# Scaling of two blocks' values on VectorE, gathers ahead of the read tree at two block ends, rows of MLP tiles 2 and 3 ahead of the last scatter

## The chip, the cores and the metric

The kernel runs on one core of a Trainium2 chip. A core has TensorE (PE in the profile) for matmuls, VectorE (DVE), ScalarE (ACT) and GpSimd (POOL) for elementwise work, and SyncE (SP), which here does nothing but issue DMAs. Each engine works through its own program in order and waits on semaphores that others raise. The metric is the device time of one execution in microseconds. Before the change it is 1930.82 us, the median of 3 runs (1924.5 to 1932.3).

## The reference

One transformer layer over x of 16 sequences of 512 tokens with 256 features. The input is normalised once to xn, and then

- out = x + attention layer(xn) + mixture of experts(xn).
- The attention layer normalises again, forms q, k, v and two gates beta and g per head (16 heads of 16), and runs a recurrence over the 512 tokens: S = S·g; S = S + beta·k (v − kᵀS)ᵀ; o = qᵀS, where k is divided by its norm. Then come the projection Wo, a residual, a layer norm and an MLP of width 1024 with gelu.
- The mixture routes each token to 8 of 64 experts (at most 128 slots an expert), each expert a gated MLP 256 → 192 → 256; the weighted rows are added per token, with a shared expert beside them.

All is float32. The recurrence is the sequential part: 512 steps, each on a state of 16 × 16 for each of 256 pairs of sequence and head.

## The kernel before, in words

**Tiles and blocks.** Time is cut into 8 blocks of 64 tokens and each block into 8 iterations of 8 steps, so the main loop runs I = 0 to 63 on every engine. The 256 pairs lie on 128 partitions in two groups G. In each iteration VectorE does the 8 steps of the recurrence (`step`, lines 1123 to 1138: four instructions for a group, eight for a step). GpSimd forms the outputs of the iteration (`reads`): a product of the states with q over half an iteration (L827, 128x2048), and then a tree of additions (L835, L836, L837, L841). Beside it one token tile of something else is carried along: for I = 1 to 16 routing, for I = 19 to 34 (X0 to X1) four experts an iteration, from I = 35 (FILL) on the MLP of 64 token tiles.

**Expert iterations.** With n = I − 19, GpSimd gathers the token rows of the next four experts (`gather(n + 1)`, L862, four indirect DMAs) at the start of its iteration, and scatters the four results of the experts by adding to DRAM (`scatter`, L869). Each scatter waits until the one before it has landed (`sc_done`). A gather waits for `slots_ready`, the slot list, which VectorE computes in `finish_round` one round an iteration at step 1, and for the four results of the iteration whose buffer it takes. TensorE multiplies, ScalarE evacuates, and VectorE forms the product of each expert's two halves (`product`, L1062) after steps 2, 3, 5 and 6. Where `summed(I)` holds, the second half of an iteration's outputs has its tree on VectorE instead (L1175, reading what GpSimd put in `rx`, L849); at the last iteration of a block (I = 23 and 31) both trees are on GpSimd.

**Block ends.** Before block k + 1 can start, its keys are scaled by the inverse norm `rk` (`key_factors`, L1045), and its values and gates are scaled: `value_factors` (L802, 128x128), `scale_values` (L808, 128x1024, one for each group) and `scale_gates` (L816, L818). GpSimd does these at j = 6 and j = 7 of the block, ahead of that iteration's reads. VectorE waits for three increments of `vals_ready` and then copies the first keys (L1056). At j = 7 GpSimd also stores the block's outputs to DRAM (`o_d`, L973), behind the trees; the first read of the next block waits until that store has landed (L825).

**The start of the MLP.** At I = 35 SyncE runs `first_rows`: it loads the rows of tiles 0 and 1 (`back_rows`: L572 from `xw_d`, L582 twice from `o_d`) and the weights w2, waits for all 64 scatters, loads the sums of tiles 0 and 1 (`back_sums`, L592), then the rows of tiles 2 and 3, and raises `rows_free`, for which the first gelu waits. TensorE's `back_attn(i)` (L1756) needs the rows of tile i; VectorE's `back_x1(i)` (L1099) takes what it gives, for tile 2 after step 2 of I = 36; `back_sum(i)` (L1106) ends a tile. GpSimd computes each tile's inverse deviation between its reads (`back_rstd`, L903, L751, L905).

The order on each engine is written out by hand in the loops. Nothing reorders it.

Of the kernel before, what the change touches and what calls it, by code (L numbers as in the profile page):

```python
# [23 lines left out]
ALU = mybir.AluOpType  # L24
# [6 lines left out]
P = 128  # L31
B, T, D = 16, 512, 256
H, DH = 16, 16
DC = D // P
BLK = 64
NBLK = T // BLK
ST = 8
NB2 = B // 2
# [113 lines left out]

def sums_on_vector(k):
    return X0 <= (k - 1) * NB2 + 3 <= X1


ROUNDS_END = R1 + NR - 1
# [19 lines left out]
def layer(nc, x, Wq, Wk, Wv, Wb, Wg, Wo, bo, ln1_g, ln1_b, ln2_g, ln2_b, w1, b1, w2, b2,  # L177
          router_wT, w_gate, w_up, w_down, ws_gate_up, ws_down, out):
    ctx = ExitStack()
    with ctx:  # L180
# [294 lines left out]
        def _(sp):  # L475
# [108 lines left out]
            def back_rows(i):  # L584
                back_rows_x(i)
                back_rows_o(i)
# [30 lines left out]
            def first_rows():  # L617

                sp.wait_ge(y_done, UNITS_R + E)
                for i in range(2):  # L620
                    back_rows(i)
                sp.dma_start(w2_s, w2.rearrange("(c p) n -> p c n", p=P)).then_inc(mlp_ld, 16)
                sp.wait_ge(sc_done, 16 * E)
                for h in range(BUF):
                    for r in range(RT):
                        sp.wait_ge(g_ld[h][r], 16 * (E // RT // 2))
                for i in range(2):
                    back_sums(i)
                for i in range(2, 4):
                    back_rows(i)  # L630
                sp.sem_inc(rows_free, 1)

            for I in range(NI):
# [69 lines left out]
        def _(pool):  # L703
# [218 lines left out]
            for I in range(NI):  # L922
                h, j, n, k, i = I % 2, I % NB2, I - X0, I // NB2 + 1, I - R0
                if I == R1:
                    g.tensor_copy(w_s[:, :, BLK], slot_col[:, 1:2].to_broadcast([P, E])).then_inc(base_ready, 1)
                if 1 <= i <= NRT:
                    residual(i - 1)
                    route_lowered(i - 1)
                back_roots(I, 0)
                if X0 <= I and I + 1 < X1:  # L930
                    gather(n + 1, (n + 1) % 2)
                if X0 < I <= X1:
                    scatter(n * RT - 1, 3, 1 - h)
                if k < NBLK and j in (3, 4) and not sums_on_vector(k):
                    square_sums(k, j - 3)
                if k < NBLK and j == 6:
                    value_factors(k)
                    scale_values(k, 0)
                if k < NBLK and j == 7:
                    scale_values(k, 1)  # L940
                    scale_gates(k)
                if X0 <= I < X1:
                    reads(I, h, 0, j, lambda: scatter(n * RT, 0, h))
                    scatter(n * RT + 1, 1, h)
                    if summed(I):
                        products(I, h)
                        scatter(n * RT + 2, 2, h)
                    else:
                        reads(I, h, 1, j, lambda: scatter(n * RT + 2, 2, h))
                else:  # L950
                    reads(I, h, 0, j, lambda: back_roots(I, 2))
                    if 1 <= i <= NRT:
                        route_weights(i - 1)
                    back_roots(I, 1)
                    if I == X0 - 1:
                        for i in range(BUF):
                            pool.wait_ge(r_stored[i], 64 * NB2)
                            pool.wait_ge(w_stored[i], 32 * NB2)
                        pool.wait_ge(zero_st, 32)
                        gather(0, 0)  # L960
                    if I + 1 < NI:
                        reads(I, h, 1, j)
                    if 1 <= I <= 1 + LATE:
                        front_factors(I + 3)
                        route_factors(I + 3)
                if h == 1:
                    relink()
                if I == NI - 1:
                    pool.wait_ge(last_read, 2)
                if j == NB2 - 1 and I < SEG[2]:  # L970
                    pool.wait_ge(x_sums, 2 * sums_before(I))
                    for s in range(2):
                        g.dma_start(o_st[I // NB2, s], oblk[:, s].rearrange("p v t -> p (v t)")).then_inc(o_stored, 16)  # L973
                if I >= SEG[2] and (I + 1) * ST % PT == 0:
                    n = (I - SEG[2]) * ST // PT
                    for s in range(2):
                        g.dma_start(ol_st[n, s], oblk_l[:, n, s].rearrange("p v t -> p (v t)")).then_inc(o_stored, 16)
# [7 lines left out]
        def _(dve):  # L985
# [61 lines left out]
            def square_sums(k, s):  # L1047

                dve.wait_ge(sq_ready, k * 2 + s + 1)
                dve.wait_ge(rk_ready, k)  # L1050
                v.tensor_reduce(n2[:, s, :], sq[:, :].rearrange("p (t d) -> p t d", d=DH), AX.X, ALU.add).then_inc(n2_ready, 1)

            def stage_keys(L, G):

# [159 lines left out]
            first_keys()  # L1214
            relink()
            t_ = [0]

            def body(I, h, at, m_):
                j = I % NB2
                dve.wait_ge(prod_done, I * 2)  # L1220
                for s in range(ST):
                    step(I, h, s, at, m_)
                    if s == 4 and j in (3, 4) and I // NB2 + 1 < NBLK and sums_on_vector(I // NB2 + 1):
                        square_sums(I // NB2 + 1, j - 3)
                    if s == 5 and j == 5 and I // NB2 + 1 < NBLK:
                        key_factors(I // NB2 + 1)
                    r = {2: 0, 3: 1, 5: 2, 6: 3}.get(s)
                    if r is not None and (R0 <= I < R1 or X0 <= I < X1):
                        product((I - R0 if I < R1 else I - X0 + NRT) * RT + r, r)
                    if 1 <= I <= 1 + LATE and s >= 5:  # L1230
                        late_stats(I + 3, s - 5, t_)
                    if s >= 6 and summed(I - 1):
                        read_sum(I - 1, s - 6)
                    if R0 + 1 <= I <= R1 and s in (0, 1, 2, 6):
                        {0: top_values, 1: top_marks, 2: top_mask, 6: top_sums}[s](I - R0 - 1)
                    if I == R1 + 1 and s == 0:
                        prefix()
                    if finish_at(I, s) is not None:
                        finish_round(finish_at(I, s))
                    if I == FILL and s == 2:  # L1240
                        dve.wait_ge(mlp_bias, 1)
                        v.tensor_tensor(b1_s[:, :], LG[:, 0:MC], b1_in[:, :], ALU.add).then_inc(mlp_bias, 1)
                    i = sum_at(I, s)
                    if i is not None:
                        back_sum(i)
                    i = x1_at(I, s)
                    if i is not None:
                        back_x1(i)
# [711 lines left out]
```

## Time and profile before

| | before |
|---|---|
| median of 3 runs | 1930.82 us |
| the profiled execution's own time | 1931.82 us |
| its span, first to last instruction | 1930.1 us |
| DVE busy | 1742.8 us, 90% |
| POOL busy | 1587.7 us, 82% |
| PE busy | 1436.1 us, 74% |
| ACT busy | 909.1 us, 47% |
| mean granted TensorE clock | 0.832 |

The durations below are from the one profiled execution. Expert iterations run from about 600 to 1110 us of its span (VectorE busy 482.26 of 510 us there), the MLP with the rest of the recurrence from there to the end.

### The profile page before, as it was taken

The numbers are of one execution on the slowest core, as the hardware profiler recorded it, in microseconds if no ns is written. First come the engines' busy times: TensorE is split into PE (matmuls) and PEld (weight loads), VectorE is DVE, ScalarE is ACT, GpSimd is POOL, SyncE is SP. The second block draws the span as 40 slices with busy tenths as digits, with TensorE's granted clock in tenths as the row PEclk, the third lists the DMA queues.
The fourth block names the chain that finished last, engine by engine and source line by source line (L and its number), as shares of the span: only waits on it lengthen the run. The fifth ranks groups of instructions, "written<-read, shape, count | busy, mean of one in ns | idle before, by whom it ended". The sixth has DMA issues, their size and how long they took to land. (4 is left out here: it accounts for less than half of the span.)

```text
span 1930.1 us, 31359 instructions
## 1 busy us (share of the span) xinstructions
PE 1436.1 (74%) x8802; PEld 1247.6 (65%) x8802; DVE 1742.8 (90%) x4967; ACT 909.1 (47%) x2609; POOL 1587.7 (82%) x1343
## 2 busy tenths in 40 slices
PE   6776777877854577667665668988898988789738
PEld 5665666766743566556554557877777877668637
DVE  3599999999999999999987988989999999988970
ACT  4545455556544644555542445555554454334303
POOL 5469999898998888788897788889898999897851
PEclk9878778878875788788776779999999999989868
DMA  8575345534456657855658322242223311111120
GB/s 174 149 178 116 69 97 125 133 75 96 95 124 150 155 132 164 217 132 130 165 132 222 74 61 64 84 118 69 57 60 102 87 54 49 57 50 49 40 53 13
DMA packets 337169, 201.24 MB, mean 104 GB/s; under 512 B 208227, under 2 KB 327717, under 8 KB 336997
## 3 DMA queue, kind: packets, MB, share of 16 engines
q1 hardware_dynamic: 318724, 168.43, 35.5%
q0 software_dynamic: 15616, 30.55, 7.2%
q8 instruction: 71, 1.16, 0.3%
q14 instruction: 102, 0.83, 0.1%
q10 hardware_dynamic: 2656, 0.26, 0.1%
HBM read 127.58 MB, written 71.60 MB: 103 GB/s over the span
## 5 line engine op out<-in xcount | busy, mean ns | idle before, releaser
L827 POOL TENSOR_TENSOR rp<-S,qs 128x2048 f32<-128x2048 f32 x113 | 519.8, 4600 | 89.3 <-DVE S L1138 63.7
L1123 DVE SCALAR_TENSOR_TENSOR vwin<-S,gwin,bank 128x256 f32<-128x256 f32 x1024 | 483.7, 472 | 0.3
L1138 DVE SCALAR_TENSOR_TENSOR S<-S,gwin,bank 128x256 f32<-128x256 f32 x1024 | 483.1, 472 | 0.3
L1128 DVE TENSOR_REDUCE nu<-vwin 128x16 f32<-128x272 f32 x1024 | 438.1, 428 | 0.3
L1132 DVE TENSOR_TENSOR bank<-nu,bank 128x256 f32<-128x256 f32 x1024 | 430.6, 421 | 0.6
L1773 PE MATMUL bank<-region 128*128 128x128 f32 x2048 | 288.2, 301 | 0.0
L1773 PEld LDWEIGHTS bank<-region 128*128 128x128 f32 x2048 | 273.1, 214 | 18.7 <-issue 18.0
L835 POOL TENSOR_TENSOR r<-rp 128x1024 f32<-128x1024 f32 x113 | 274.3, 2428 | 7.0
L1653 PE MATMUL bank<-xaT,wqkvg 128*128 128x128 f32 (+1 forms) x1792 | 242.1, 288 | 11.1 <-ACT xaT L1312 8.0
L1784 PE MATMUL bank<-region 128*128 128x256 f32 x1024 | 234.7, 383 | 0.0
L1653 PEld LDWEIGHTS bank<-xaT,wqkvg 128*128 128x128 f32 (+1 forms) x1792 | 216.2, 190 | 25.5 <-ACT xaT L1312 11.6
L1462 ACT ACTIVATE region<-bank,b_s 128x128 f32<-128x128 f32 x512 | 145.0, 364 | 176.3 <-PE bank L1773 176.0
L1784 PEld LDWEIGHTS bank<-region 128*128 128x128 f32 x1024 | 193.2, 194 | 24.4
L1688 PE MATMUL bank<-gT,region 128*96 128x128 f32 x1024 | 156.6, 317 | 56.4 <-ACT gT L1392 42.4
L1688 PEld LDWEIGHTS bank<-gT,region 128*96 128x96 f32 x1024 | 144.0, 196 | 72.0 <-ACT gT L1392 53.4
L1397 ACT ACTIVATE sgu<-bank 96x256 f32<-96x256 f32 x128 | 48.6, 380 | 232.6 <-PE bank L1688 223.1
L1688 PE MATMUL bank<-gT,wsgu_s 128*96 128x128 f32 x1024 | 151.0, 311 | 0.0
L836 POOL TENSOR_TENSOR r<-r 128x512 f32<-128x512 f32 x113 | 143.5, 1270 | 8.9
L869 POOL DMA_INDIRECT acc_d<-region,idx_i x64 | 101.7, 1589 | 53.0 <-issue 37.0
L1688 PEld LDWEIGHTS bank<-gT,wsgu_s 128*96 128x96 f32 x1024 | 140.0, 193 | 0.0
L1324 ACT ACTIVATE stg<-bank 128x128 f32<-128x128 f32 x384 | 76.5, 282 | 117.8 <-PE bank L1653 108.5
L1697 PE MATMUL bank<-region,hg_s 96*128 96x256 f32 x256 | 78.5, 434 | 47.9 <-DVE hg_s L1062 36.4
(158 smaller groups left out, 2329.6 us busy)
## 6 DMA issues: line engine op xcount, KB each, us to landing
qkv_d<-stg SPq DMA_DIRECT2D x192, 128.0 KB, 2.3
region<-in_L_ffn_w_gate SPq DMA_DIRECT2D x64, 192.0 KB
region<-in_L_ffn_w_up SPq DMA_DIRECT2D x64, 192.0 KB
region<-in_L_ffn_w_down SPq DMA_DIRECT2D x64, 192.0 KB
region<-in_L_attn_x SPq DMA_DIRECT2D x16, 512.0 KB, 7.6
region<-in_L_attn_x SPq DMA_DIRECT2D x32, 256.0 KB, 4.8
xw_d<-region SPq DMA_DIRECT2D x32, 256.0 KB, 3.5
acc_d<-region SPq DMA_DIRECT2D x32, 256.0 KB, 4.1
```

The lines of the kernel that those rows point to most:

```text
L827: g.tensor_tensor(rp[:, :, :].rearrange("p (a v) d -> p a v d", v=DH), S[h][:, lo:lo + HS].rearrange("p t s (v d) -> p (t s) v d", v=DH), ...
L835: link(g.tensor_tensor(r1[:, :, :], rp[:, :, 0:8], rp[:, :, 8:16], ALU.add))
L836: link(g.tensor_tensor(r1[:, :, 0:4], r1[:, :, 0:4], r1[:, :, 4:8], ALU.add))
L1123: m[G] = mark(v.scalar_tensor_tensor(products_of(I, s, G)[0], earlier(h, s, G).rearrange("p (v d) -> p v d", v=DH), gwin[:, I // NB2 & 1, ...
L1128: m[G] = mark(v.tensor_reduce(nu[:, G], products_of(I, s, G)[1], AX.X, ALU.add))
L1132: m[G] = mark(v.tensor_tensor(outer[G].rearrange("p (v d) -> p v d", v=DH), nu[:, G].unsqueeze(2).to_broadcast([P, DH, DH]), key(s, G), AL ...
L1138: ins = v.scalar_tensor_tensor(S[h][:, s, G], earlier(h, s, G), gwin[:, I // NB2 & 1, G, 1, t:t + 1], outer[G], ALU.mult, ALU.subtract)
L1462: last = a_.activation(mid[i % 2][:, m, :], (G0, G1)[half][:, n * P:(n + 1) * P], ACT.Gelu, bias=b1_s[:, m:m + 1])
L1653: last = mm(dst[0:n, :], wqkvg[:, c, i * P:i * P + n], xaT[h][:, c, :], start=(c == 0), stop=(c == DC - 1))
L1688: last = mm(bk[0:FH, i * P:(i + 1) * P], w[:, c, (i % 2) * FH:(i % 2 + 1) * FH], gT[:, c, :], start=(c == 0), stop=(c == DC - 1))
L1773: last = mm((G0, G1)[half][:, n * P:(n + 1) * P], w1_s[:, c, m * P:(m + 1) * P], hT[i % 2][:, c, :], start=(c == 0), stop=(c == DC - 1))
L1784: last = mm(out_bank(i)[:, 0:D], mid[i % 2][:, m, :], w2_s[:, m, :], start=(m == 0), stop=(m == MC - 1))
```

## The change

Three edits. First, `values_on_vector(k)` is true for k = 3 and 4: for these blocks the five scaling instructions leave GpSimd and are issued by VectorE at j = 6 (I = 22 and I = 30), after steps 3, 4, 5 and 6. Second, at I = 23 and I = 31 GpSimd gathers for the experts two iterations on, between the product of its second read and the tree, and the gather at the start of I = 24 and I = 32 goes. Third, `first_rows` loads the rows of tiles 0 to 3 before it waits for the last scatter. To do so it waits first for the gathers of even n, whose buffers tiles 2 and 3 take, and only later for those of odd n.

```diff
+def values_on_vector(k):
+    return X0 <= (k - 1) * NB2 + 6 and k * NB2 <= X1
...
                 sp.wait_ge(y_done, UNITS_R + E)
-                for i in range(2):
+                for r in range(RT):
+                    sp.wait_ge(g_ld[0][r], 16 * (E // RT // 2))
+                for i in range(4):
                     back_rows(i)
                 sp.dma_start(w2_s, w2.rearrange("(c p) n -> p c n", p=P)).then_inc(mlp_ld, 16)
                 sp.wait_ge(sc_done, 16 * E)
-                for h in range(BUF):
-                    for r in range(RT):
-                        sp.wait_ge(g_ld[h][r], 16 * (E // RT // 2))
+                for r in range(RT):
+                    sp.wait_ge(g_ld[1][r], 16 * (E // RT // 2))
                 for i in range(2):
                     back_sums(i)
-                for i in range(2, 4):
-                    back_rows(i)
                 sp.sem_inc(rows_free, 1)
...
-                if X0 <= I and I + 1 < X1:
+                if X0 <= I and I + 1 < X1 and (j or I == X0):
                     gather(n + 1, (n + 1) % 2)
...
-                if k < NBLK and j == 6:
+                if k < NBLK and j == 6 and not values_on_vector(k):
                     value_factors(k)
                     scale_values(k, 0)
-                if k < NBLK and j == 7:
+                if k < NBLK and j == 7 and not values_on_vector(k):
                     scale_values(k, 1)
                     scale_gates(k)
...
-                        reads(I, h, 1, j, lambda: scatter(n * RT + 2, 2, h))
+                        def rows_ahead():
+                            scatter(n * RT + 2, 2, h)
+                            if I + 2 < X1:
+                                gather(n + 2, n % 2)
+                        reads(I, h, 1, j, rows_ahead)
...
+            def value_work(k, part, c):
+
+                bw, gw = gwin[:, k & 1, :, 0], gwin[:, k & 1, :, 1]
+                if part == 0:
+                    for s in range(2):
+                        dve.wait_ge(*window_in(k, s))
+                    c[0] = mark(v.tensor_tensor(bw, bw, rk[:, :, :], ALU.mult))
+                    c[1] = mark(v.tensor_tensor(rk[:, :, :], rk[:, :, :], gw, ALU.mult))
+                elif part < 3:
+                    s = part - 1
+                    vw = vwin[:, k & 1, s, :, DH:DH + BLK]
+                    dve.wait_ge(vch, c[0])
+                    v.tensor_tensor(vw, vw, gwin[:, k & 1, s, 0].unsqueeze(1).to_broadcast([P, DH, BLK]),
+                                    ALU.mult).then_inc(vals_ready, 1)
+                else:
+                    dve.wait_ge(vch, c[1])
+                    dve.wait_ge(vals_ready, k * 3 + 2)
+                    v.tensor_tensor(bw, bw, rk[:, :, :], ALU.mult).then_inc(vals_ready, 1)
...
+                    if j == 6 and 3 <= s <= 6 and I // NB2 + 1 < NBLK and values_on_vector(I // NB2 + 1):
+                        value_work(I // NB2 + 1, s - 3, w_)
```

GpSimd's program before, from the second read of I = 23 to the first read of I = 24 (rp is the product, r1 the tree, o_d the block's store, xw_d the gathers, acc_d a scatter):

```order
L827 TENSOR_TENSOR rp<-S1,qs1 128x2048
L869 DMA acc_d<-region,idx_i 8320x256
L835 TENSOR_TENSOR r1<-rp 128x1024
L836 TENSOR_TENSOR r1<-r1 128x128x4
L837 TENSOR_TENSOR r1<-r1 128x128x2
L841 TENSOR_TENSOR oblk<-r1 128x16x4 x2
L714 ISA
L973 DMA o_d<-oblk 128x1024 x2
L862 DMA region<-xw_d,idx_i 128x320 x4
L869 DMA acc_d<-region,idx_i 8320x256
L827 TENSOR_TENSOR rp<-S0,qs0 128x2048
```

The same piece of GpSimd's program after:

```order
L830 TENSOR_TENSOR rp<-S1,qs1 128x2048
L872 DMA acc_d<-region,idx_i 8320x256
L865 DMA region<-xw_d,idx_i 128x320 x4
L838 TENSOR_TENSOR r1<-rp 128x1024
L839 TENSOR_TENSOR r1<-r1 128x128x4
L840 TENSOR_TENSOR r1<-r1 128x128x2
L844 TENSOR_TENSOR oblk<-r1 128x16x4 x2
L717 ISA
L980 DMA o_d<-oblk 128x1024 x2
L872 DMA acc_d<-region,idx_i 8320x256
L830 TENSOR_TENSOR rp<-S0,qs0 128x2048
```

The four gathers moved up past the tree and the store, so that now only one scatter stands between the store and the read that waits for it.

VectorE's program after, around step 3 of I = 22 (the rows with gwin and rk are new; hg_s is the product for the second expert):

```order
L1154 TENSOR_REDUCE nu<-vwin 128x16
L1066 TENSOR_TENSOR gwin<-gwin,rk 128x2x64
L1067 TENSOR_TENSOR rk<-rk,gwin 128x128
L1088 TENSOR_TENSOR hg_s1<-sgu1,bank6 96x256
L1149 SCALAR_TENSOR_TENSOR vwin<-S0,gwin,bank0 128x16x16
L1158 TENSOR_TENSOR bank2<-nu,bank2 128x256
```

Two instructions are put ahead of the product; the two of 128x1024 and the last small one stand in the same way after steps 4, 5 and 6.

SyncE's program before, at I = 35 (xw_d and o_d are the rows of a tile, w is w2, acc_d the sums):

```order
L572 DMA region<-xw_d 128x1x256
L582 DMA region<-o_d 128x2x64 x2
L572 DMA region<-xw_d 128x1x256
L582 DMA region<-o_d 128x2x64 x2
L622 DMA region<-in_L_attn_w 128x8x256
L592 DMA region<-acc_d 128x1x256 x2
L572 DMA region<-xw_d 128x1x256
L582 DMA region<-o_d 128x2x64 x2
L572 DMA region<-xw_d 128x1x256
L582 DMA region<-o_d 128x2x64 x2
L486 DMA xt<-in_L_attn_x 128x1x256
```

In the changed program the last two pairs of L572 and L582 stand ahead of the load of w2, and the wait for the scatters, which is in front of L592, is behind all four.

## Rows read from the trace of the kernel before

**Rows 1.** The page's first part: busy us (share of the span) xinstructions.
```profile
PE 1436.1 (74%) x8802; PEld 1247.6 (65%) x8802; DVE 1742.8 (90%) x4967; ACT 909.1 (47%) x2609; POOL 1587.7 (82%) x1343
```

**Rows 2.** Waits of VectorE over the span: us in total, times, longest us.
```profile
DVE region L1106 <- PE bank L1784: 53.2, 16, 7.1
DVE region L1099 <- PE bank L1757: 38.2, 10, 10.2
...
DVE bank L1056 <- POOL gwin L818: 6.0, 1, 6.0
DVE oblk L1175 <- POOL rx L849: 2.9, 3, 1.5
```

**Rows 3.** Groups of GpSimd, 700 to 760 us: busy us, mean ns, idle before.
```profile
L808 POOL TENSOR_TENSOR vwin<-vwin,gwin 128x1024 f32<-128x1024 f32 x2 | 5.3, 2652 | 0.1
...
L802 POOL TENSOR_TENSOR gwin<-gwin,rk 128x128 f32<-128x128 f32 x1 | 1.0, 1029 | 0.0
```

**Rows 4.** Groups of VectorE over the span, shapes apart.
```profile
L1132 DVE TENSOR_TENSOR bank<-nu,bank 128x256 f32<-128x256 f32 x1024 | 430.6, 421 | 0.6
...
L1210 DVE TENSOR_TENSOR win_k<-win_k,rk 128x1024 f32<-128x1024 f32 x2 | 2.4, 1222 | 0.0
```

**Rows 5.** Timeline, VectorE's copies and GpSimd: start us, us, instruction.
```profile
159.38 0.17 DVE L1031 COPY var<-region 128x8 f32<-128x8 f32 x1
...
220.64 1.17 DVE L1031 COPY var<-region 128x8 f32<-128x8 f32 x1
...
220.51 1.27 POOL L836 TENSOR_TENSOR r<-r 128x512 f32<-128x512 f32 x1
```

**Rows 6.** Timeline of I = 22, GpSimd and VectorE (end of step 4).
```profile
713.49 1.03 POOL L802 TENSOR_TENSOR gwin<-gwin,rk 128x128 f32<-128x128 f32 x1
...
716.95 4.52 POOL L827 TENSOR_TENSOR rp<-S,qs 128x2048 f32<-128x2048 f32 x1
...
714.70 0.43 DVE L1128 TENSOR_REDUCE nu<-vwin 128x16 f32<-128x272 f32 x1
```

**Rows 7.** Timeline at ends of blocks: [idle before <- what ended it].
```profile
755.28 0.64 DVE L1056 COPY bank<-win_k 128x128 f32<-128x128 f32 x2
...
760.80 5.10 POOL L827 TENSOR_TENSOR rp<-S,qs 128x2048 f32<-128x2048 f32 x1
...
1017.19 1.21 POOL L973 DMA_DIRECT2D o_d<-oblk  x2 [1.27 <-issue]
...
1024.89 5.09 POOL L827 TENSOR_TENSOR rp<-S,qs 128x2048 f32<-128x2048 f32 x1
...
1240.69 1.25 POOL L973 DMA_DIRECT2D o_d<-oblk  x2 [0.66 <-POOL oblk L841]
...
1248.22 4.54 POOL L827 TENSOR_TENSOR rp<-S,qs 128x2048 f32<-128x2048 f32 x1 [4.43 <-issue]
```

**Rows 8.** Timeline of I = 33: SyncE's first expert weights, VectorE's first product.
```profile
1024.03 0.47 SPq L564 DMA_DIRECT2D region<-in_L_ffn_w_gate  x1
...
1035.79 0.42 DVE L1062 TENSOR_TENSOR hg_s<-sgu,bank 96x256 f32<-96x256 f32 x1 [9.29 <-ACT sgu L1397]
```

**Rows 9.** Timeline of the first MLP tiles, all engines.
```profile
1108.67 1.56 POOL L869 DMA_INDIRECT acc_d<-region,idx_i  x1 [3.08 <-issue]
...
1113.54 1.65 SPq L572 DMA_DIRECT2D region<-xw_d  x1
...
1116.67 0.69 PE L1762 MATMUL bank<-ident,region 128*128 128x128 f32 x2 [13.95 <-ACT region L1446]
1124.46 2.07 PE L1756 MATMUL bank<-wo_s,region 128*128 128x256 f32 x4 [7.10 <-DMA region<-o_d]
...
1127.72 0.42 DVE L1099 TENSOR_TENSOR region<-bank,region 128x256 f32<-128x256 f32 x1 [7.22 <-PE bank L1757]
...
1136.32 0.19 POOL L903 TENSOR_SCALAR region<-region 128x1 f32<-128x1 f32 x1 [2.60 <-ACT region L1440]
...
1165.42 0.42 DVE L1106 TENSOR_TENSOR region<-bank,region 128x256 f32<-128x256 f32 x1 [5.00 <-PE bank L1784]
```

More of the change, by code:

```diff
@@ L1216, in _ @@
             t_ = [0]
+            w_ = [0, 0]
             def body(I, h, at, m_):
```

## The prediction

> **What bounds the kernel now.** I read the page's busy shares first: VectorE 90%, GpSimd 82% [rows 1]. VectorE carries the recurrence, so what counts is each place where it waits, and I read its waits next. In the expert part it waits little: once 6.0 us for GpSimd's last scaling instruction, at the end of the block at I = 31, and three times, 2.9 us together, for the product that it sums itself [rows 2]. In the MLP part it waits 53.2 and 38.2 us for TensorE [rows 2]. Then I read the timelines of all engines around the three edited places. The reader is to see in them that GpSimd runs behind VectorE in the expert part (its second read of I = 23 starts at 760.80, 5.5 us after VectorE began the next block at 755.28 [rows 7]), and that in the MLP part the engines wait in a ring: VectorE for TensorE, ScalarE for GpSimd's deviations, GpSimd for ScalarE and for VectorE's states. A gain there counts only as far as both VectorE and GpSimd have it.
>
> **Edit 1, the scaling.** It takes off GpSimd, for each block, two instructions of 128x1024 and three of 128x128: 5.3 + 1.0 us [rows 3], and for the other two small ones about 0.9 (no more than the 1.0 of the first each), together 7.2 us. It puts them on VectorE. The trace has the large form there at 1.22 us [rows 4]. It has no small one; from 0.42 us for 256 elements and 1.22 for 1024 [rows 4] the slope is 1.04 ns an element, and 128 elements come to 0.29. So a block costs 2 × 1.22 + 3 × 0.29 = 3.3 us, both 6.6 us. VectorE is without a gap there, so nothing hides this.
>
> That price is for an idle GpSimd. VectorE's copies in SBUF show another one: the copy of 8 elements takes 0.17 us, but the one that began at 220.64, just behind the start of a GpSimd addition at 220.51, took 1.17 and ended at 221.81, where the addition ended too (220.51 + 1.27 = 221.78) [rows 5]. The recurrence's own instructions show no such stretching: the 1024 of L1132 have a mean of 0.42 us [rows 4], and they take one input from PSUM. The new ones take both inputs from SBUF. The row nearest to them in engine and memories is the stretched copy, so I price each as waiting until the GpSimd instruction then running has ended. The bounds from rows: none waits (0), or each of the eight places waits for a whole read product of 4.52 us [rows 6] (36 us for both blocks). For the value between I lay them on the timeline. At I = 22 step 4 ends at 714.70 + 0.43, to which the first two add 0.6. GpSimd, rid of the scaling, starts its read product at about 713.5 instead of 716.95 and ends it at about 718.0 [rows 6]. The large instruction there waits about 3 us, the one after step 5 falls into the tree and waits up to 1.3, and the last one meets either the gap at the next scatter or the next product. That is about 4 us for the block; the same for the second makes S = 8 us in all. The two small ones ahead fall into the issue of gathers, and I count nothing.
>
> The Trainium skill states this lock in "SBUF — State Buffer", section "Who interferes with whom": a VectorE instruction with two SBUF inputs and a GpSimd instruction that reads SBUF exclude each other for the whole of the one that came first. The trace agrees for copies (1.17 against 0.17 us), and no row has a VectorE instruction with two SBUF inputs beside a busy GpSimd. By that page the sum is the one below; were it for copies alone, it would be the first rival.
>
> What edit 1 takes off VectorE: the 6.0 us at I = 32 and the 2.9 us of the summed products, 8.9 in all, if GpSimd is at least as early relative to VectorE as now, which it is, since VectorE is later and GpSimd does less. VectorE enters the MLP part at 6.6 + S − 8.9 = S − 2.3, later by 5.7 us.
>
> **Edit 2, the gathers.** They are not what VectorE waits for. The longest wait in this part, 9.29 us at I = 33, looks like a late gather, but the expert's weights were only issued at 1024.03 and the product came 11.8 us later [rows 8]: SyncE had waited for the slot list that VectorE finishes in that same iteration. That chain starts from VectorE and moves with it, so I leave the 9.3 us in place. What the edit costs is cover. The store of the block's outputs is waited for by the next read; where no gathers stand between, at 1240.69, the read started 7.5 us after the store's issue, 4.43 of them idle [rows 7]. At I = 32 the read started 7.7 us after the store (1017.19 to 1024.89), filled with gathers and a scatter, without idle time [rows 7]. Some 5 of the 6.5 us between them are the four gathers. After the change the store is issued these 5 us later relative to the reads ahead of it, and the wait for it shows: GpSimd's read comes up to 5 us later at I = 24 and I = 32. The scatter behind that read had waited for its predecessor, which stood behind four gathers; of that I estimate about 3 us to come back. I count +2 for GpSimd at each.
>
> **GpSimd's side of edits 1 and 2.** At the first block its 7.2 us hardly count: the second read of I = 23 cannot start before VectorE has finished the block, and that is later by 3.3 + 4 us, so the read moves from 760.80 to about 763 (+2.3). At the second block it is behind VectorE by more than it gains and keeps its gain, less the scatters' waits that the scaling had covered: about −5. With the two losses of 2 and what went before, the last scatter stands within about 1 us of 1108.67 [rows 9]. For S = 0 the same working gives −5, for S = 17 about +5: some 0.6 us for each of S.
>
> **Edit 3, the rows.** TensorE's first matmul of tile 2 waited 7.10 us for rows that SyncE issued at 1113.54, behind the last scatter, and VectorE waited 7.22 us for it [rows 9]. With the rows loaded ahead of the last scatter, what is late next is TensorE's transpose of tile 0 at 1116.67, which waits for ScalarE and so for GpSimd [rows 9]: the matmul follows at 1117.4 and its sum is there at about 1121, as VectorE arrives (1127.72 − 7.22 = 1120.5). So VectorE gains 7 us there even if GpSimd gains nothing; it then reaches the sum of tile 1 (1165.42, waited 5.00) earlier. GpSimd's part is smaller: its wait of 2.60 at 1136.32 for ScalarE goes [rows 9]. The sum at 1165.42 comes when both sides are there: VectorE's side gives S − 2.3 − 7.2 − 5.0 = S − 14.5 (−6.5 for S = 8), GpSimd's −5 + 0.6 S − 2.6 = −7.6 + 0.6 S (−2.8). The later one decides: −3 us. Behind it the ring passes the shift on to the end; I give it no further gain or loss.
>
> The sum: 1931.8 (the profiled execution's own time) − 2.8 = 1929; that execution was 1.0 us over the median of the runs, so I say 1928.
>
> **Rivals.**
> - No port wait (S = 0). For it: all rows of such instructions on VectorE have their plain duration [rows 4]; against: they ran beside an idle GpSimd, and the copy [rows 5]. It gives −7.6: 1923.
> - Port waits at long products. Place: the eight instructions at I = 22 and 30. Past S = 13 the sum turns to slower than before (−7.6 + 0.6 × 13 = 0). With whole products of 4.52 met at five of eight places S is 22, and both sides are late: VectorE +7.5, GpSimd +5.6: 1938. For it: GpSimd's read now starts just ahead of step 4's end [rows 6]. Against: the tree's additions are short (1.27 us for the one in [rows 5]), and between them and the products stand the issues of scatters.
> - The MLP part gives more. VectorE's 53.2 + 38.2 us of waits there [rows 2] depend on how the engines are staggered; with SyncE free earlier at I = 35, by the loads of two tiles, the ring may tighten by another 5 to 8 us: 1921, or 1919 with few port waits. Against: only the first tiles' rows were behind the scatter.
> - Edit 3 changes nothing that counts, because the wait passes over to ScalarE and GpSimd (14 us wait at 1116.67 [rows 9]) and the 5.00 at 1165.42 grows by what was gained: GpSimd's 2.6 is lost too, 1931 to 1933.
>
> **How the numbers follow.** Forecast 0.42, no port wait 0.22, long port waits 0.14, more from the MLP part 0.14, edit 3 without effect 0.08. A change under 0.5% (9.7 us) cannot be told from none here. Faster by more needs less than 1921.2: nearly all of the third rival's case, the lower half of the second case's spread of some 3 us, little else: 0.28. Slower by more needs over 1940.5: part of the long waits: 0.11. The rest, 0.61, is within. The likeliest case's own range is 1924 to 1932; the range for 8 in 10 reaches to the other cases, 1917 to 1937.
>
> **What the changed profile would show.** Right: the 6.0 us wait for gwin gone; the two large scalings on VectorE at I = 22 and 30 with means well over 1.22 us and ends that coincide with ends of GpSimd's instructions; GpSimd idle some 3 to 5 us between the store and the first read of I = 24 and 32; the 9 us wait at I = 33 still there; tile 2's L1099 without its 7 us, and a wait of several us left at the sum of tile 1. Wrong: scalings at 1.22 us (first rival), the wait at I = 33 gone with the earlier gathers (then edit 2 is worth up to 9 us and my reading of the weights fails), or a shift at the end that differs from the shift at 1165 by over 4 us.

## The result and the profile after

The changed kernel takes 1936.01 us (median of 20 runs, 1929.12 to 1941.72) against 1930.27 us (20 runs of the kernel before on the same chip): ratio 1.0026, 95% interval [1.0014, 1.0039], about 5 us slower. The forecast was 1928. The profiled execution took 1935.86 us, 4.0 more than before; its span is 1934.1 us, its mean granted clock 0.828 against 0.832.

The busy times, for [rows 1]:

```profile
PE 1442.8 (75%) x8802; PEld 1253.8 (65%) x8802; DVE 1758.3 (91%) x4977; ACT 909.2 (47%) x2609; POOL 1579.3 (82%) x1333
```

VectorE has 15.5 us more work. GpSimd is busy 8.4 us less, though its groups of scaling instructions are 14.3 us shorter (14.4 was the forecast).

Waits of VectorE over the span, for [rows 2]:

```profile
DVE region L1132 <- PE bank L1813: 56.2, 16, 7.1
...
DVE region L1125 <- PE bank L1786: 31.7, 10, 10.1
DVE hg_s L1088 <- ACT sgu L1426: 22.8, 16, 8.4
```

The 6.0 us for gwin and the 2.9 for rx are gone, as forecast. TensorE's share fell by 6.5 us at L1125 (tile 2) and grew by 3.0 at L1132.

The scalings, now on VectorE, in the timeline (start, us, instruction), for [rows 3 to 6]:

```profile
711.90 0.28 DVE L1066 TENSOR_TENSOR gwin<-gwin,rk 128x128 f32<-128x128 f32 x1
712.10 0.28 DVE L1067 TENSOR_TENSOR rk<-rk,gwin 128x128 f32<-128x128 f32 x1
715.55 5.34 DVE L1072 TENSOR_TENSOR vwin<-vwin,gwin 128x1024 f32<-128x1024 f32 x1
723.74 2.08 DVE L1072 TENSOR_TENSOR vwin<-vwin,gwin 128x1024 f32<-128x1024 f32 x1
...
951.64 6.13 DVE L1072 TENSOR_TENSOR vwin<-vwin,gwin 128x1024 f32<-128x1024 f32 x1
960.61 1.21 DVE L1072 TENSOR_TENSOR vwin<-vwin,gwin 128x1024 f32<-128x1024 f32 x1
```

and GpSimd beside the first two:

```profile
714.71 5.09 POOL L830 TENSOR_TENSOR rp<-S,qs 128x2048 f32<-128x2048 f32 x1
719.97 2.40 POOL L872 DMA_INDIRECT acc_d<-region,idx_i  x1 [0.17 <-issue]
721.83 2.90 POOL L838 TENSOR_TENSOR r<-rp 128x1024 f32<-128x1024 f32 x1
724.80 2.14 POOL L839 TENSOR_TENSOR r<-r 128x512 f32<-128x512 f32 x1
```

The scaling begun at 715.55 ends at 720.89, 1.09 us behind the product's end at 719.80, where the whole instruction takes 1.22 beside an idle GpSimd. Over 1.22 us, the four large ones took 4.12, 0.86, 4.91 and 0 us more; with 0.3 for one small one S, the port waits of edit 1 taken together, is 10.2 us (8 forecast). It works the other way too: the addition at 724.80 took 2.14 us where the mean of its kind is 1.28, the scatter's issue at 719.97 took 2.40 where its mean is 1.61, and at I = 30 a scatter and a gather were held up as well:

```profile
956.85 2.38 POOL L872 DMA_INDIRECT acc_d<-region,idx_i  x1 [0.17 <-issue]
...
960.85 1.82 POOL L865 DMA_INDIRECT region<-xw_d,idx_i  x1 [0.31 <-issue]
```

Together that is 3.3 us of GpSimd's time.

The ends of the two blocks on GpSimd, and of one in the MLP part, for [rows 7]:

```profile
764.93 4.52 POOL L830 TENSOR_TENSOR rp<-S,qs 128x2048 f32<-128x2048 f32 x1 [1.20 <-DVE S L1164]
...
783.66 1.17 POOL L980 DMA_DIRECT2D o_d<-oblk  x2 [0.95 <-POOL oblk L844]
788.90 4.52 POOL L830 TENSOR_TENSOR rp<-S,qs 128x2048 f32<-128x2048 f32 x1 [2.12 <-issue]
...
1026.77 1.18 POOL L980 DMA_DIRECT2D o_d<-oblk  x2 [0.64 <-POOL oblk L844]
1031.37 4.50 POOL L830 TENSOR_TENSOR rp<-S,qs 128x2048 f32<-128x2048 f32 x1 [1.47 <-issue]
...
1242.76 1.25 POOL L980 DMA_DIRECT2D o_d<-oblk  x2 [0.66 <-POOL oblk L844]
1250.46 4.54 POOL L830 TENSOR_TENSOR rp<-S,qs 128x2048 f32<-128x2048 f32 x1 [4.59 <-issue]
```

The first reads of I = 24 and 32 start 6.6 and 6.5 us later than before, with idle time of 2.12 and 1.47 us in front of them that was not there (3 to 5 were forecast). Some of every such difference is older than the edits: VectorE starts I = 18, where none of the three has begun, 1.0 us later in this trace than in the one before. Where two traces are compared below, I take that difference off and say so.

The expert part's end and the first MLP tiles, for [rows 8, 9]:

```profile
1032.55 0.47 SPq L568 DMA_DIRECT2D region<-in_L_ffn_w_gate  x1
1043.38 0.42 DVE L1088 TENSOR_TENSOR hg_s<-sgu,bank 96x256 f32<-96x256 f32 x1 [8.36 <-ACT sgu L1426]
...
1112.55 1.56 POOL L872 DMA_INDIRECT acc_d<-region,idx_i  x1 [2.94 <-issue]
1120.57 0.69 PE L1791 MATMUL bank<-ident,region 128*128 128x128 f32 x2 [10.32 <-ACT region L1475]
1122.12 2.04 PE L1785 MATMUL bank<-wo_s,region 128*128 128x256 f32 x4 [0.86 <-ACT region L1481]
1127.96 0.40 DVE L1125 TENSOR_TENSOR region<-bank,region 128x256 f32<-128x256 f32 x1
...
1138.04 0.19 POOL L906 TENSOR_SCALAR region<-region 128x1 f32<-128x1 f32 x1 [0.25 <-POOL oblk L844]
...
1167.50 0.42 DVE L1132 TENSOR_TENSOR region<-bank,region 128x256 f32<-128x256 f32 x1 [5.63 <-PE bank L1813]
```

Edit 3 did its part: TensorE no longer waits for rows and VectorE not at all at tile 2. But GpSimd reaches this place late (the last scatter at 1112.55, before 1108.67; 2.9 us with the difference at I = 18 taken off), and the wait passes to tile 1's sum. Where did the 14.3 us go that it was relieved of? Its waits from VectorE's start of I = 22 to that of I = 36 tell it (us in total, times, longest):

```profile
POOL acc_d L872 <- issue: 29.5, 39, 4.2
...
POOL acc_d L872 <- DMA acc_d<-region,idx_i: 8.6, 5, 3.1
POOL rx L852 <- DVE S L1164: 5.8, 1, 5.8
POOL acc_d L872 <- POOL oblk L844: 5.7, 7, 0.9
POOL rp L830 <- issue: 3.6, 2, 2.1
...
POOL region L865 <- DVE idx_i L1219: 1.5, 1, 1.5
POOL rp L830 <- DVE S L1164: 1.2, 1, 1.2
```

In front of scatters it waited 46.9 us in all, as much as before (46.8, of which 33.6 in the row that answers to the first). New are 5.8 + 3.6 + 1.2 for VectorE's states and the store, and 1.2 more for the slot list: 11.8 us. The stretched instructions above take another 3.3. So 14.3 us were gained and some 15 lost; of the 2.9 us by which the last scatter is late, about 2 stand in no row.

### The profile page after: what moved, and what is told of

It reads as the page before. It is cut to its first block and busy times, and to the rows that moved or that the text cites. A ratio compares the mean times of both kernels' runs of the same rounds, so it can differ in the third digit from the quotient of the medians.

```text
span 1934.1 us, 31359 instructions
## 1 busy us (share of the span) xinstructions
PE 1442.8 (75%) x8802; PEld 1253.8 (65%) x8802; DVE 1758.3 (91%) x4977; ACT 909.2 (47%) x2609; POOL 1579.3 (82%) x1333
```

## The experiments

Sixteen kernels, each against the kernel before on the same chip; "us" is (ratio − 1) × 1930, and the half width of its interval is 2 to 5 us. e1 to e8 ran on one chip, e9 to e12 on a second, f1 to f4 on a third; a difference of two rows carries the intervals of both. Edit 1P is edit 1 with the products of gates and norm kept in PSUM (below); M moves GpSimd's wait for the store.

| kernel | edits | median us | ratio [95%] | us |
|---|---|---|---|---|
| changed | 1, 2, 3 | 1936.0 | 1.0026 [1.0014, 1.0039] | +5.0 |
| e1_psum | 1P, 2, 3 | 1929.2 | 0.9993 [0.9982, 1.0004] | −1.4 |
| e2_no_values | 2, 3 | 1932.0 | 1.0014 [1.0002, 1.0026] | +2.7 |
| e3_no_gathers | 1, 3 | 1929.4 | 0.9993 [0.9979, 1.0008] | −1.4 |
| e4_rows_only | 3 | 1927.2 | 0.9987 [0.9978, 0.9997] | −2.5 |
| e5_psum_rows | 1P, 3 | 1917.6 | 0.9960 [0.9938, 0.9982] | −7.7 |
| e6_gathers_only | 2 | 1933.6 | 1.0029 [1.0018, 1.0041] | +5.6 |
| e7_store_late | 1, 2, 3, M | 1923.0 | 0.9971 [0.9958, 0.9984] | −5.6 |
| e8_weights_first | 3, weights | 1930.5 | 1.0002 [0.9987, 1.0016] | +0.4 |
| e9_psum_rows_store | 1P, 3, M | 1913.0 | 0.9917 [0.9892, 0.9941] | −16.0 |
| e10_all_psum_store | 1P, 2, 3, M | 1923.1 | 0.9948 [0.9930, 0.9967] | −10.0 |
| e11_base_store | M | 1920.8 | 0.9947 [0.9931, 0.9962] | −10.2 |
| e12_all_blocks | 1P for five blocks, 3, M | 1923.2 | 0.9961 [0.9938, 0.9984] | −7.5 |
| f1_gathers_behind_tree | as e10, gathers behind the tree | 1923.1 | 0.9961 [0.9948, 0.9975] | −7.5 |
| f2_gathers_first_block | as e10, edit 2 at I = 23 alone | 1922.8 | 0.9959 [0.9944, 0.9975] | −7.9 |
| f3_gathers_second_block | as e10, edit 2 at I = 31 alone | 1915.6 | 0.9927 [0.9913, 0.9941] | −14.1 |
| f4_delay | as e9, 2.9 us of work added twice | 1921.8 | 0.9957 [0.9944, 0.9970] | −8.3 |

**e1, the port wait.** The product of beta and rk goes to PSUM (`bwp`), so the large scalings and the last small one get one input from there:

```diff
-                    c[0] = mark(v.tensor_tensor(bw, bw, rk[:, :, :], ALU.mult))
+                    c[0] = mark(v.tensor_tensor(bwp, bw, rk[:, :, :], ALU.mult))
...
-                    v.tensor_tensor(vw, vw, gwin[:, k & 1, s, 0].unsqueeze(1).to_broadcast([P, DH, BLK]),
+                    v.tensor_tensor(vw, vw, bwp[:, s].unsqueeze(1).to_broadcast([P, DH, BLK]),
...
-                    v.tensor_tensor(bw, bw, rk[:, :, :], ALU.mult).then_inc(vals_ready, 1)
+                    v.tensor_tensor(bw, bwp, rk[:, :, :], ALU.mult).then_inc(vals_ready, 1)
```

> The changed kernel, but the product of beta and rk goes to a free corner of a PSUM bank and the value scalings and the last gate product read it from there, so that each has one input in SBUF; the count of instructions is the same. Theory (ports: two inputs in SBUF wait for GpSimd's instruction; in the changed kernel the large ones take 5.34, 2.08, 6.13 and 1.21 us): all four large ones at 1.2 us, VectorE some 9 us earlier by I = 32 than in the changed kernel, and the time 5 to 8 us under it, near or a little under the kernel before. Rival (the instruction is slow there for its own sake, by its shape or by what lies around it): durations stay at 2 to 6 us and the time stays at the changed kernel's. Rival (edits 1's port waits are covered, GpSimd decides): durations fall, the time does not.

In its timeline all four take 1.20 us, beside the same kinds of instruction on GpSimd (three of them):

```profile
712.94 1.20 DVE L1074 TENSOR_TENSOR vwin<-vwin,bank 128x1024 f32<-128x1024 f32 x1
716.99 1.20 DVE L1074 TENSOR_TENSOR vwin<-vwin,bank 128x1024 f32<-128x1024 f32 x1
943.20 1.20 DVE L1074 TENSOR_TENSOR vwin<-vwin,bank 128x1024 f32<-128x1024 f32 x1
```

The same instruction, one input in another memory: 1.20 instead of 5.34 and 6.13 us. The kernel gains 6.4 us (1.0026 to 0.9993), and from e3 to e5 (0.9993 to 0.9960) it is the same 6.4. The PSUM form takes away some 10 us of S and with them GpSimd's 3.3; for each us of S 0.6 to 0.7 reach the end, close to the slope of 0.6 that the prediction used, though with GpSimd's part in it and with intervals of 2 to 4 us it is no precise test of it.

**e2 to e4, one edit left out or one alone.** e2 has `values_on_vector` return False; e3 has the gathers back at the start of I = 24 and 32; e4 has both.

> The changed kernel without edit 1: scalings on GpSimd, the gathers ahead of the tree and the rows ahead of the last scatter stay. Theory (edit 1 with its port waits makes it slower, edit 3 gives a few us, edit 2 little): VectorE waits some 10 us for the gates at I = 32, since GpSimd has the gathers and the scalings ahead of it; the time is 3 to 6 us under the kernel before. Rival (edit 2 is what costs, by the store's wait that shows): the time is at or over the kernel before.

> The changed kernel without edit 2: the gathers stand again at the starts of I = 24 and I = 32, behind the store. Theory (edit 1 costs, edit 2 does little): port waits as before the undoing, 8 to 12 us in all, and a time within 3 us of the changed kernel. Rival (edit 2 costs because GpSimd's read then waits for the store, 2.1 and 1.5 us seen): 3 to 5 us under the changed kernel. Rival (edit 2 is the one that gives): slower than the changed kernel by 3 us or more.

> The kernel before with edit 3 alone. Theory: the wait of 7.2 us for tile 2 goes, the one for the sum of tile 1 (5.0) grows by what GpSimd does not gain, so VectorE enters I = 38 2 to 4 us earlier and the time is 2 to 5 us under the kernel before. Rival (edit 3 gives its 7 us whole): 6 to 8 us under. Rival (it gives nothing, the ring waits for GpSimd): within 1 us.

Edit 3 alone is worth 2.5 us. Its trace has VectorE 7.45 us earlier at the start of I = 37 (difference at I = 18 taken off), but only 2.8 from I = 38 on: the wait at tile 1's sum grew from 5.00 to 7.69 us, and what stayed is near the 2.6 forecast for GpSimd. Edit 1 costs 1.2 us (e3 against e4) or 2.3 (changed against e2), neither clear of zero with these intervals. Edit 2 costs 5.2 (e2 against e4) or 6.4 (changed against e3).

**e5 and e6, edit 2 taken away and alone.**

> The changed kernel without edit 2, and with edit 1 in the form whose products of gates and norm lie in PSUM, so that the two large scalings have one input from PSUM. Theory (edit 2 costs GpSimd 5 to 6 us, edit 1 without port waits is free or better): the sum of the parts, 1924 to 1926, 4 to 6 us under the kernel before; scalings of 1.2 us; GpSimd's shift at I = 36 about -6. Rival (edit 1 costs by VectorE's work alone, whatever the memories): 1927 to 1928, as with the rows alone.

> The kernel before with edit 2 alone. Theory (the store's landing is no longer covered): 1934 to 1937, 4 to 6 us over the kernel before, with GpSimd's first reads of I = 24 and 32 late by 5 or more and idle time of 4 to 6 us in front of them. Rival (edit 2 costs only beside edit 1, because both delay the same block ends): within 1.5 us of the kernel before.

e6 costs 5.6 us: edit 2 needs no other edit to do harm. (Its one profile shows less than 1 us of it at the end; a single profiled execution does not resolve such differences.) In e6's timeline the exposed wait is plain, 5.17 and 3.60 us:

```profile
777.23 1.17 POOL L981 DMA_DIRECT2D o_d<-oblk  x2 [0.65 <-POOL oblk L845]
785.52 4.53 POOL L831 TENSOR_TENSOR rp<-S,qs 128x2048 f32<-128x2048 f32 x1 [5.17 <-DMA acc_d<-region,idx_i]
1021.76 1.18 POOL L981 DMA_DIRECT2D o_d<-oblk  x2 [0.65 <-POOL oblk L845]
1028.49 4.49 POOL L831 TENSOR_TENSOR rp<-S,qs 128x2048 f32<-128x2048 f32 x1 [3.60 <-issue]
```

e5's median is below the 1924 to 1926 that the parts promised, though by the ratio (7.7 us, 4.2 either way) the surplus is not clear. Its GpSimd waits in the same stretch as above show where it keeps what the changed kernel loses: the scatters 45.8 us, as before, and nothing for the store, with 0.3 for VectorE's states:

```profile
POOL acc_d L872 <- issue: 22.6, 36, 6.2
POOL region L865 <- issue: 13.7, 45, 0.3
POOL acc_d L872 <- DMA acc_d<-region,idx_i: 13.1, 7, 3.0
POOL acc_d L872 <- POOL oblk L844: 8.0, 10, 0.8
...
POOL rx L852 <- DVE S L1164: 0.3, 1, 0.3
```

Here GpSimd keeps all that it was relieved of (its last scatter is issued at 1093.28), and the trace ends 13.9 us earlier than before, the difference at I = 18 taken off. That is more than the 7.7 us of the timed runs, which reach from 1909 to 1934 us.

**e7, is the store's wait the cost of edit 2?** In the changed kernel the wait is moved behind the product, which does not write the stored buffer:

```diff
-                if half == 0:
-                    pool.wait_ge(o_stored, min(I >> 3, NBLK - 1) * OST)
                 pool.wait_ge(act_staged, I + 1)
                 g.tensor_tensor(
                     rp[:, :, :].rearrange("p (a v) d -> p a v d", v=DH),
...
+                if half == 0:
+                    pool.wait_ge(o_stored, min(I >> 3, NBLK - 1) * OST)
                 o, t0 = read_cols(I)
```

> The changed kernel, but GpSimd waits for the landing of a block's store ahead of the tree's last additions, which write the stored buffer, and no longer ahead of the read product, which does not touch it. Theory (the wait for the store is what edit 2 costs): the idle time in front of the first reads of I = 24 and 32 goes, and with it the 4 us waits of the later blocks; 1929 to 1931, 5 to 7 us under the changed kernel. Rival (edit 2 costs because the gathers stand ahead of the tree and delay the outputs and the store themselves): the wait moves but the time stays over 1934.

10.6 us under the changed kernel, more than any theory had. The idle time is gone everywhere, as at I = 32 and I = 40:

```profile
1018.22 1.18 POOL L980 DMA_DIRECT2D o_d<-oblk  x2 [0.65 <-POOL oblk L844]
...
1020.77 5.11 POOL L828 TENSOR_TENSOR rp<-S,qs 128x2048 f32<-128x2048 f32 x1
...
1232.13 1.25 POOL L980 DMA_DIRECT2D o_d<-oblk  x2 [0.66 <-POOL oblk L844]
1235.21 4.53 POOL L828 TENSOR_TENSOR rp<-S,qs 128x2048 f32<-128x2048 f32 x1
```

It looked like a proof, and was not one: it lacked the control without edit 2, which follows.

**e8, the wait at I = 33.** `mlp_load()` now stands behind `experts(I - X0)` in SyncE's loop.

> The kernel before with edit 3, and with SyncE's loads of expert weights at I = 32 issued ahead of the MLP weights that stood in front of them. It tells what the wait of 8 to 9 us at I = 33 hangs on. Theory (the weights, issued late by SyncE): the wait shrinks by 2 us or more, though the expert product that follows may wait for other things; the time 0 to 2 us under that with the rows alone (1925 to 1927). Rival (the gather or the slot list itself): the wait stays at 8 to 9 us and the time at 1927.

The weights are issued at 1007.93 and the wait shrinks to 6.01 us, so it is the weights' wait, and the earlier gathers never touched it. The time does not fall, it is 2.9 us over e4 (the two intervals make that barely clear): VectorE is 6.5 us earlier at I = 34 and has 1.9 of it left at I = 36.

**e9 to e12, combinations.**

> Edit 1 in its PSUM form and edit 3, without edit 2, and with the wait for the block's store moved behind the product. Theory (the wait for the store is covered by the four gathers where edit 2 is left out, and counts only at blocks 5 to 7, in the MLP part): between 1 and 5 us under the same kernel without the moved wait (1917.6), so 1913 to 1917. Rival (what the moved wait gave beside edit 2 was the gathers' own earliness, so without edit 2 it gives nothing): 1917 to 1919.

> All three edits, edit 1 in its PSUM form, and the wait for the store moved behind the product. Theory (beside the wait for the store, edit 2 costs nothing and gives nothing): within 2 us of the kernel without edit 2 and with the moved wait. Rival (the gathers ahead of the tree also delay the block's outputs and so GpSimd's second half): 3 us or more over it.

> The kernel before, and the wait for the store moved behind the product: none of the three edits. Theory: at I = 24 and 32 there is no idle time to take (the gathers cover it), at I = 40, 48 and 56 there are some 4 us each, of which GpSimd's side in the MLP part passes on a part: 2 to 6 us under the kernel before. Rival (in the MLP part both sides wait for TensorE, so that the time at GpSimd is free): within 1.5 us of it.

> As the kernel with edits 1 (PSUM form) and 3 and the moved wait, but with VectorE scaling values and gates of blocks 3 to 7 instead of 3 and 4. Theory (in the MLP part GpSimd's side decides at block ends too, and VectorE waits there for TensorE): each further block gives GpSimd 7 us and costs VectorE 3.3, of which a part reaches the end: 3 to 10 us less. Rival (there VectorE's side decides, since it is busy 91% of the span): 2 us or more over it.

The moved wait gives 10.2 us to the kernel before, 8.3 to e5 (e9), 8.7 to e1 (e10) and 10.6 to the changed kernel (e7): the same with and without edit 2. At the block ends that edit 2 does not touch the kernel before idles 0.55, 0.45, 4.43, 2.14 and 5.86 us, 13.4 in all. The traces locate only the last of these on VectorE: I = 57 takes it 24.5 us in all nine with the moved wait and 27.8 to 28.8 in all nine without. That is some 4 us of the 8 to 10; where the rest comes in they do not show. So the store's wait is visible in edit 2's traces, but it is not what edit 2 costs: with the wait moved, edit 2 still costs 6.0 us (e10 against e9, each 2 to 5 us either way; f1 to f4 below repeat it with narrower intervals). e9 is 16 us under the kernel before and some 21 under the changed one. Of e12 the rival was right: scaling on VectorE in the MLP part as well costs 8.5 us more than it gives (e12 against e9).

**f1 to f4, what is left of edit 2.** f1 issues the gathers directly ahead of the store, behind the tree; f4 has GpSimd repeat the tree's first addition (L835 before) at the start of I = 24 and 32, which holds up the scatter behind it by 2.9 us each time:

```diff
+                if X0 < I <= X1 and j == 0:
+                    link(g.tensor_tensor(r1[:, :, :], rp[:, :, 0:8], rp[:, :, 8:16], ALU.add))
                 if X0 < I <= X1:
                     scatter(n * RT - 1, 3, 1 - h)
```

> All three edits, edit 1 in its PSUM form and the wait for the store moved, but the four gathers stand behind the tree and only ahead of the store, where edit 2 has them ahead of both. Theory (the gathers ahead of the tree delay the tree and start 1.5 us too early for the slot list): the cost of edit 2 goes, 1912 to 1916, as with the gathers behind the store. Rival (the later store is the cost): it stays, 1919 to 1924.

> Edit 1 in its PSUM form, edit 3, the wait for the store moved, and edit 2 at I = 23 alone. Theory (the wait for the slot list at I = 23 and the later scatters enlarge the delay until I = 31): most of edit 2's cost, 1917 to 1922. Rival (the second block end, whose delay enters the MLP part directly): 1912 to 1915.

> The same with edit 2 at I = 31 alone. Theory (first block): 1912 to 1915. Rival (second block): 1917 to 1922. If both block ends cost half, this and the kernel with I = 23 alone both come to 1915 to 1918.

> Edit 1 in its PSUM form, edit 3 and the moved wait, no edit 2; instead GpSimd repeats one addition of 128x1024 (2.9 us, its result is overwritten later) at the start of I = 24 and of I = 32. Theory (delays of GpSimd at a block's end are enlarged by the scatters behind them, in the trace 2.6 us grew to 8.3 between I = 24 and 30): 7 us or more over the kernel without it (1913), so 1920 or more. Rival (GpSimd's delay is passed on one to one): 4 to 6 us, 1917 to 1919. Third (its waits take the delay up): within 2 us of 1913.

Not the tree: f1 is as slow as e10 within the intervals (theory wrong; f1's rival, that the later store is the cost, fits its time but is not tested apart, since in e10, f1 and f2 the gathers stand ahead of the store too). Not the second block: f3 is only 1.9 us over e9, less than e9's interval. The cost sits at I = 23: f2 is 6.2 us over f3 on one chip, with intervals that do not meet, and 8.1 over e9.

How it gets from there to the end is only partly seen. At I = 23 the gathers come too early for the slot list, in e10:

```profile
764.40 1.01 POOL L865 DMA_INDIRECT region<-xw_d,idx_i  x1 [1.54 <-DVE idx_i L1221]
```

But f2 has no such wait and costs as much, so it is not the cause. And a small lag grows. GpSimd's first read is later in f2 than in f3 (difference at I = 18 taken off) by 1.0 us at I = 23, 1.1 at I = 24, 1.7 at I = 28, 4.4 at I = 30 and 7.4 at I = 31. The first of these is ahead of the moved gathers, so it is not theirs; and the growth falls where the two programs are the same. It comes in front of scatters, 56.4 us in f2 and 47.3 in f3 (I = 22 to 35), mostly at the first scatter behind an iteration's first read. At I = 30, in f2 and then in f3:

```profile
960.89 1.60 POOL L872 DMA_INDIRECT acc_d<-region,idx_i  x1 [3.24 <-issue]
951.84 1.60 POOL L872 DMA_INDIRECT acc_d<-region,idx_i  x1 [0.17 <-issue]
```

That scatter waits until the one before it, issued right behind four gathers, has landed. In f3 this landing took 7.1 to 7.3 us at I = 26 to 29 but 4.2 and 3.8 at I = 30 and 31; in f1, which is slow, 6.2 and 7.8 at I = 30 and 31 (f2's trace has no landings). Why it is long in one kernel and short in the other stays open.

f4 shows that plain delay costs too: 5.8 us of it cost 5.8 against f3 and 7.7 against e9. Both fit a delay passed on one to one (the rival's 4 to 6) as well as an enlarged one (the theory's 7 or more); the intervals, 4 to 5 us either way for these differences, do not part them.

## Why the prediction was wrong

The change is under 0.5%, the outcome given 0.61, and the time lies in the range; but the range reached well to both sides of "no change", and the sign is wrong: −2.8 forecast, +5.0 measured. The rival of long port waits gives 1938, near the 1936 measured, but not by what happened: it needs an S of 22, and S was 10.2. Point by point:

- **Port waits:** the mechanism held and its size nearly, S = 10.2 for 8 (the prediction's own rows give 2.3 us for the first wait, which it rounds to 3), and a slope of about 0.6 to the end is in keeping with e1 (6.4 of some 10 us). What it left out is the other direction, 3.3 us on GpSimd. The rival without a port wait is ruled out by 5.34 and 6.13 us. The trace agrees with the section of the Trainium skill that was weighed, "Who interferes with whom" in "SBUF — State Buffer", and e1 with its converse: one input from PSUM, no exclusion (1.20 us at all four places).
- **Edit 3:** right in size and reason. −2.5 us (−2.6 forecast as GpSimd's part), the 5.00 grew to 7.69, GpSimd's side decided.
- **The wait at I = 33:** right, 8.36 us left, and e8 ties it to the weights.
- **Edit 1's gain on GpSimd: the term that turned the sign.** "At the second block it is behind VectorE by more than it gains and keeps its gain", "about −5"; with the first block's delay the prediction has edit 1 at some −3 to −4. Timed, it measures +1.2 to +2.3, so this term is 4 to 6 of the 7.8 us between −2.8 and +5.0. The traces of e3 and e4 differ by edit 1 alone (difference at I = 18 taken off): GpSimd is later in e3 by 1.7 us at the second read of I = 23, where 2.3 was forecast. So the first block went as foreseen, and the 5.8 us wait for VectorE's states only spends what the prediction had written off there. But it is later by 3.6 us at I = 24, 3.8 at I = 30 and still 2.2 at the last scatter: the second block gave back 1.6 us, not 5, and some 2 were lost on the way there, where the prediction had nothing. The port's hold on GpSimd (3.3 us) is one part of what is missing; what took the rest is open. In PSUM form, without port waits, edit 1 measures −5.2 (e5 against e4) with edit 3 alone and −4.1 (e1 against e2) beside edit 2.
- **Edit 2: mis-sized as well, and in the wrong place.** "I count +2 for GpSimd at each" block, after 3 us that come back: +4; measured 5.2 to 6.4 us in five pairs. The reads did come late with idle time in front, as forecast, but the scatters' waits in I = 22 to 35 stayed at 46.9 us where some 6 less were counted for this edit alone. And the first block carries nearly all of the cost, not through the wait for the store: with that wait moved it costs as much.
- The ring of the MLP part passed the shift on, mostly: +1.1 us at tile 1's sum (2.1 in the timeline, less the 1.0 at I = 18), +3.1 at the end of the trace.

The wait for the store, whose moving gives more than any of the three edits (10.2 us in e11), stood in the prediction's own rows: the 4.43 us in front of 1248.22 [rows 7] were read as a hint for edit 2 and not as a cost of the kernel before.

## What to carry to other kernels

Before moving elementwise work from one of two engines that share SBUF to the other, put one operand in PSUM or count the lock on both sides; the engine that is relieved keeps its gain only as far as it is not already waiting for the one that is loaded. Place a wait ahead of the instruction that needs it, not at the head of the group. A wait that becomes visible where a change was made is not yet that change's cost: take it away in the kernel without the change as well. And one profiled execution shows where time goes, but not a difference of some 5 us in 1930: that takes timed runs.

## What the runs showed of the hardware

The lock between the two engines stretches also GpSimd's issue of a DMA: 2.40 and 2.38 us for two scatters (mean 1.61) and 1.82 for a gather (mean 0.99), each beside a VectorE instruction with two SBUF inputs.

A scatter issued right behind four gathers lands after 3.8 us in one place and after 8.7 in another (f3 at I = 31, f1 at I = 28).

VectorE's instructions are not always of one length. In the profiles of e9 to e12, taken one after the other, the product of 128x256 (L1132 before, there 421 ns) is longer in most stretches; in e9 by group:

```profile
L1158 DVE TENSOR_TENSOR bank<-nu,bank 128x256 f32<-128x256 f32 x1024 | 457.3, 447 | 0.6
```

and 461 to 472 ns on average between 1300 and 1700 us. In the profiles of all other kernels it is 412 to 435 ns in every stretch of 100 us. These four are also the only experiments that ran on the second chip, so the chip and the hour cannot be told apart; what sets the length no run shows. No verdict above rests on positions in these four traces alone.
